# Attention written out batch by batch, values projected with tokens on the output partitions, gate products in two halves of the array

## The chip, the cores and the metric

The kernel runs on one core of a Trainium2 chip. The metric is the device time of one execution in microseconds (us); the median of several executions is compared. The engines are TensorE (PE, with its weight loads as PEld), VectorE (DVE), ScalarE (ACT), GpSimd (POOL) and SyncE (SP), which here issues DMAs.

## What is computed

Two layers on x of 8 batches x 512 tokens x 256, all in float32. `ctx` has the same shape. Each layer adds a mixer with the context and then a feed-forward part:

```python
x = x + mlstm_mix(layernorm(x), ctx, ctx, gates, outnorm)      # 4 heads of 64
x = x + gelu(layernorm(x) @ w1 + b1) @ w2 + b2                 # 256 -> 1024 -> 256
x = x + attention(layernorm(x), ctx, ctx, Wq, Wk, Wv, Wo, Bq, Bk, Bv, Bo)
x = x + expert_mlp(layernorm(x), gate_w, w1, w2)               # 8 experts, 512 tokens each

# attention: 16 heads of 64
q = query @ Wq + Bq; k = key @ Wk + Bk; v = value @ Wv + Bv     # each 256 -> 1024
probs = softmax(q_h @ k_h.T / 8)                               # per batch and head, 512 x 512
out = concat_h(probs @ v_h) @ Wo + Bo

# gates of the mixer, before the recurrence over tokens
igate = concat(q, k, v) @ ig_kernel + ig_bias                  # 4 heads, q = layernorm(x), k = v = ctx
fgate = concat(q, k, v) @ fg_kernel + fg_bias
```

## The kernel before, in words

The engines' programs are written out by hand, with semaphores between them. The stages follow each other with a barrier between: `setup` (constants), `mlstm_gates` (loads x and ctx, turns both so that features lie on partitions, gate products), `mix_and_mlp` (mixer and feed-forward part, straight code, batch by batch), `attention`, `logits`, `router`, `experts`.

**Gate stage.** PE transposes context and normalized x of a batch (`turn`, L216 and L224), ACT copies both out of PSUM, and `gate_maps` (L234) multiplies 64 columns of gate weights with 512 tokens, four steps of 128 features. The weights of batch i are shifted so that its 8 gate rows fall on rows of their own; all batches accumulate into the same 64 rows of one PSUM bank. Batch i is turned ahead of the gate product of batch i-1. At the end ACT reads rows 32 to 63 and 0 to 31 with the bias (L274, L276), and DVE and ACT work through a chain of row operations of 32x512 (L323 to L341) to the end of the stage. DVE's statistics (L58) and the normalization (L73) feed the transposes; the reciprocal root is POOL's (L85).

**Attention.** A unit u is one batch and one pair of heads, 64 in all; the pair changes slowest (`b = u % B`). The work of a unit goes in steps j = 0 to 7 (head j // 4, 128 queries each):
- PE: the score of step j (L925, two fp32r products with 512 columns), the transposes (L936) of the probabilities of step j-2 (at j = 0 and 1 those of steps 6 and 7 of the unit before). After them come, at j = 0, 1 and 4, the query, key and value products of unit u+1 (L906); at j = 2 the products of values and probabilities of unit u-1 (L947, the two heads on two halves of the array's columns); at j = 5 and 6 the output products (L957); at j = 7 the transposes of the values of unit u+1 (L914).
- DVE: row maximum (L1071), reciprocal of the row sum (L1076), copies of turned probabilities (L1083), the low parts of queries and keys (L1054, L1061); at j = 7 the two additions to x (L1089) and the copy of the turned values (L1066).
- ACT: exponential (L1015), queries and keys with bias (L990, L997), values with bias (L1003), the copy of the heads' output (L1010), and two of eight copies of turned probabilities (L1027).
- POOL: scales the probabilities (L1044).
- SP: copies the keys within the on-chip memory, four transfers of 256 KB a unit (L876), once ACT and DVE have written both parts.

There are two score banks in PSUM, so the score of step j waits for the exponential of step j-2. Queries and values share bank 4; keys and turned values share bank 5.

The weights of one pair of heads are on chip at a time. SP loads the next pair's into `w_next` and `b_next`, and every eight units DVE copies and scales them (`switch_weights`, L1093 to L1096), for which PE's next query product waits. The units run in hardware loops on every engine (`every_unit`), so their addresses and semaphore counts are computed from loop registers.

```python
for j in range(NBL):                       # PE, unit u
    score(u, par, j, first); turn(u, j - 2, first)     # at j < 2: turn(u - 1, 6 + j)
    if j in (0, 1, 4): project(u + 1, min(j, 2))
    if j == 2: weigh_values(u - 1, ...)
    if j in (5, 6): output(u - 1, j - 5)
    if j == 7: turn_values(u + 1)
```

## Time and profile before

| | us |
|---|---|
| median of 3 executions | 2006.98 |
| lowest and highest | 1998.52, 2008.62 |
| the profiled execution | 2001.98 |
| its span, first to last instruction | 2000.3 |
| gate stage, to DVE's last instruction | 73.1 |
| mixer and feed-forward part, to the next stage's first issue | 459.55 |
| attention, to DVE's last addition | 1690.8 |

The stages' ends are read from the timeline. The page gives for each engine its busy time, its share of the span and the number of instructions; a granted clock of 1.00 is 2.4 GHz for PE, 0.50 is 1.2 GHz. Ends of matmuls are modelled, so the distance from start to start tells more than a duration. A float32 product is two PE instructions, a float32 transpose and an fp32r product are one.

### The profile page before, as it was taken

Reading aid. Unit: us, or ns where it says so; the run is one execution under the profiler, and the core shown is the slowest. Engines: PE = TensorE matmul, PEld = TensorE weight load, DVE = VectorE, ACT = ScalarE, POOL = GpSimd, SP = SyncE. Lnnn points to the kernel's source line nnn. Section 1 sums busy time; section 2 is a strip of 40 time slices with the busy share of each in tenths; the row PEclk is TensorE's granted clock in tenths of the full one; section 3 lists DMA queues with packets and bytes.
Section 4 is the critical chain, followed back from the end, with each engine's and each line's share of the span. In section 5 each row is a group of like instructions: output and inputs, shape, how many; then the busy total and the mean of one; then the engine's idle time right before and its main releaser. Section 6 shows DMA issues by size and latency. Waiting matters only on the chain. (4 is left out here: it accounts for less than half of the span.)

```text
span 2000.3 us, 29128 instructions
## 1 busy us (share of the span) xinstructions
PE 1750.8 (88%) x8415; PEld 1135.9 (57%) x8415; DVE 1257.7 (63%) x2832; ACT 846.0 (42%) x1870; POOL 644.8 (32%) x761
## 2 busy tenths in 40 slices
PE   7579999995999999999999999999999997721674
PEld 4356777673666666666566566566566564721453
DVE  5444544424777777777777777777777775567341
ACT  3324333423555555555555555555555552200211
POOL 2153444421222232232232222222222222102675
PEclk9769999997999999999999999999999998555877
DMA  7000000003213213213223223223222221501443
GB/s 240 11 22 11 12 11 1 1 0 79 64 43 72 63 42 71 63 42 71 58 47 71 58 47 71 58 46 71 59 46 63 60 46 27 169 0 43 81 80 53
DMA packets 71815, 108.51 MB, mean 54 GB/s; under 512 B 16712, under 2 KB 54096, under 8 KB 71760
## 3 DMA queue, kind: packets, MB, share of 16 engines
q1 hardware_dynamic: 65616, 99.29, 20.2%
q0 software_dynamic: 6144, 8.52, 2.7%
q8 instruction: 29, 0.48, 0.1%
q14 instruction: 26, 0.21, 0.0%
HBM read 27.84 MB, written 12.85 MB: 20 GB/s over the span
## 5 line engine op out<-in xcount | busy, mean ns | idle before, releaser
L1044 POOL TENSOR_SCALAR at_Pr<-at_Pr,at_rinv 128x512 f32<-128x512 f32 x512 | 354.2, 692 | 867.6 <-DVE at_rinv L1076 867.6
L1015 ACT ACTIVATE at_Pr<-at_ps,at_nmax 128x512 f32<-128x512 f32 x512 | 351.9, 687 | 546.3 <-DVE at_nmax L1071 464.0
L925 PE MATMUL at_ps<-at_k,at_q 128*128 128x512 f32 x1024 | 439.7, 510 | 7.2 <-DMA at_k<-at_k_own 4.8
L1071 DVE TENSOR_REDUCE at_nmax<-at_ps 128x1 f32<-128x512 f32 x512 | 353.1, 690 | 114.6 <-PE at_ps L925 104.7
L936 PE MATMUL at_ps<-k_ident,at_Pr 128*128 128x128 f32 x2048 | 307.8, 273 | 4.2 <-POOL at_Pr L1044 4.2
L936 PEld LDWEIGHTS at_ps<-k_ident,at_Pr 128*128 128x128 f32 x2048 | 250.5, 140 | 84.4 <-issue 18.8
L925 PEld LDWEIGHTS at_ps<-at_k,at_q 128*128 128x128 f32 x1024 | 179.4, 191 | 157.2 <-issue 95.9
L1083 DVE COPY at_PT<-at_ps 128x512 f32<-128x512 f32 x384 | 261.0, 680 | 0.0
L906 PE MATMUL at_ps<-m_ctxT,at_w 128*128 (+1 forms) x512 | 242.2, 595 | 0.3 <-DVE at_q L1054 0.3
L947 PE MATMUL at_ps<-at_PT,at_V 128*64 128x512 f32 x1024 | 237.2, 606 | 0.9 <-DVE at_PT L1083 0.9
L1076 DVE RECIPROCAL at_rinv<-at_rsum 128x1 f32<-128x1 f32 x512 | 83.2, 163 | 179.3 <-ACT at_Pr L1015 177.3
L906 PE MATMUL at_ps<-m_xnT,at_w 128*128 (+1 forms) x256 | 126.4, 618 | 24.4 <-DVE at_w L1096 24.4
L947 PEld LDWEIGHTS at_ps<-at_PT,at_V 128*64 128x64 f32 x1024 | 68.5, 138 | 124.0 <-issue 122.9
L957 PE MATMUL at_ps<-at_wo,at_oT 128*128 (+1 forms) x512 | 131.7, 380 | 0.7 <-ACT at_oT L1010 0.7
L906 PEld LDWEIGHTS at_ps<-m_ctxT,at_w 128*128 128x128 f32 x512 | 88.1, 192 | 64.2 <-issue 62.8
L428 PE MATMUL mm_ps<-mx_w,mm_hT 128*128 128x256 f32 x512 | 120.9, 382 | 0.0
L418 PE MATMUL mm_ps<-m_xnT,mx_w 128*128 128x512 f32 x256 | 114.2, 605 | 1.3 <-ACT m_xnT L571 1.3
L428 PEld LDWEIGHTS mm_ps<-mx_w,mm_hT 128*128 128x128 f32 x512 | 93.8, 190 | 16.6 <-issue 5.3
L1054 DVE SCALAR_TENSOR_TENSOR at_q<-at_ps,at_b,at_q 64x512 fp32r<-64x512 f32 x128 | 96.0, 750 | 8.6 <-ACT at_q L990 5.7
L1015 ACT ACTIVATION_READ_ACCUMULATOR at_Pr<-at_ps,at_nmax 128x1 f32 x512 | 98.7, 193 | 0.0
L990 ACT ACTIVATE at_q<-at_ps,at_b 64x512 fp32r<-64x512 f32 x128 | 86.7, 677 | 17.9 <-PE at_ps L906 17.1
L957 PEld LDWEIGHTS at_ps<-at_wo,at_oT 128*128 128x128 f32 x512 | 87.4, 191 | 8.2 <-ACT at_oT L1010 1.6
(245 smaller groups left out, 2049.1 us busy)
## 6 DMA issues: line engine op xcount, KB each, us to landing
at_k<-at_k_own SPq DMA_DIRECT2D x256, 256.0 KB, 4.3
k_x<-in_x SPq DMA_DIRECT2D x8, 512.0 KB, 8.6
mg_ctx<-in_ctx SPq DMA_DIRECT2D x8, 512.0 KB, 8.7
mx_ctxn<-in_ctx SPq DMA_DIRECT2D x8, 512.0 KB, 3.6
rows<-lo_xn SPq DMA_DIRECT2D x8, 512.0 KB, 3.0
out<-k_x SPq DMA_DIRECT2D x1, 4096.0 KB, 14.7
ex_w_in<-in_L_ffn_w SPq DMA_DIRECT2D x16, 256.0 KB, 2.9
mx_w<-in_L_ffn_w SPq DMA_DIRECT2D x2, 1024.0 KB, 10.0
```

Source lines behind the costliest of these rows:

```text
L418: ins = pe.matmul(ps[:, H_BANK + f % 4, :], w1_s[:, k, P * f:P * f + P], xnT_all[:, k, b * S:b * S + S], start=k == 0, stop=k == DC - 1)
L428: ins = pe.matmul(ps[:, Y_BANK + t // 2, D * (t % 2):D * (t % 2) + D], hT[:, f, P * t:P * t + P], w2_s[:, f, :], start=f == 0, stop=f == F ...
L906: ins = pe.matmul(ps[:, A_BANK + k % 2, :], w_s[:, k, d, :], src[:, d, ds(b * S, S)], start=d == 0, stop=d == DC - 1)
L925: ins = pe.matmul(ps[:, S_BANK + j % 2, :], q2[:, par, h, q:q + P], k2[:, par, h, part, :], start=part == 0, stop=part == 1)
L936: ins = pe.transpose(ps[:, T_BANK + j % 2, P * t:P * t + P], Pr[:, j % 4, P * t:P * t + P], c["ident"][:, :])
L947: ins = pe.matmul(ps[AD * h:AD * h + AD, O_BANK, :], V[:, par, t, AD * h:AD * h + AD], PT[:, par, h, t, :], start=t == 0, stop=t == TPB - 1)
L957: ins = pe.matmul(ps[:, Y_BANK - half, D * (t % 2):D * (t % 2) + D], oT[:, P * t:P * t + P], wo_s[:, ds(u // B, 1), :].rearrange("p a d -> ...
L1015: act.activation(Pr[:, j % 4, :], ps[:, S_BANK + j % 2, :], ACT.Exp, bias=nmax[:, j % 4:j % 4 + 1], accum_out=rsum[:, j % 4:j % 4 + 1]).th ...
L1044: pool.tensor_scalar(Pr[:, j % 4, :], Pr[:, j % 4, :], rinv[:, j % 4:j % 4 + 1], 1.0, ALU.mult, ALU.mult).then_inc(s["pn"], 1)
L1054: ins = dve.scalar_tensor_tensor(out=q2[other, par, h, :], in0=ps[own, A_BANK, :], scalar=b_s[own, 0:1], in1=q2[own, par, h, :], op0=ALU.a ...
L1071: dve.tensor_reduce(nmax[:, j % 4:j % 4 + 1], ps[:, S_BANK + j % 2, :], AX.X, ALU.max, negate=True).then_inc(s["nmax"], 1)
L1083: dve.tensor_copy(PT[:, par, j // TPB, :, q:q + P], ps[:, T_BANK + j % 2, :].rearrange("p (t q) -> p t q", t=TPB)).then_inc(s["pt_v"], 1)
```

## The change

- Gates: `gate_maps` takes a pair of batches; the even one's product goes to PSUM rows 0 to 63, the odd one's to rows 64 to 127, in turn. DVE adds the second half's rows to fg and ig before it uses them.
- Weights: the first pair's query, key and value weights and all biases are loaded at the start of `mix_and_mlp` (`load_first`); those of the other seven pairs at the start of `attention`, in three transfers ahead of the output weights. DVE scales the query weights twice in all. `w_next`, `b_next` and `switch_weights` are gone.
- Order: the pair of heads changes fastest (`b, hp = u // HP, u % HP`), and all 64 units are straight code on every engine.
- Values: the context is the stationary operand and the weights move, so that tokens lie on the output partitions: eight products with 128 columns take the place of two with 512. The four transposes L914, ACT's copy to `vT` and DVE's copy L1066 are gone; ACT copies the bank to V at j = 5. The value bias is added to the heads' output instead (the probabilities of a row sum to 1).
- Waits: PE waits for the additions to x before `weigh_values`, DVE for its own earlier additions before the next.
- The zeros for the spare rows are written in `logits` instead of `setup`.

```diff
-                def gate_maps(i):
+                def gate_maps(pair):
+                    pe.wait_ge(s["ctxT"], 2 * pair + 2)
+                    pe.wait_ge(s["xnT"], 2 * pair + 2)
                     for k in range(2 * DC):
+                        for half in range(2):
+                            i = 2 * pair + half
+                            rhs = (xnT_all if k < DC else ctxT_all)[:, k % DC, i * S:i * S + S]
+                            at = R - MH - MH * i
+                            out = slice(2 * R * half, 2 * R * half + 2 * R)
+                            ins = pe.matmul(ps[out, GATE_BANK, :], gate_w[:, k, at:at + 2 * R], rhs,
+                                            start=pair == 0 and k == 0, stop=i >= B - 2 and k == 2 * DC - 1)
...
                 turn(0)
+                turn(1)
                 pe.wait_ge(s["gw"], 5)
-                for i in range(1, B):
-                    turn(i)
-                    gate_maps(i - 1)
-                gate_maps(B - 1)
+                for pair in range(1, B // 2):
+                    turn(2 * pair)
+                    gate_maps(pair - 1)
+                    turn(2 * pair + 1)
+                gate_maps(B // 2 - 1)
...
                 dve.wait_ge(s["fg"], 1)
+                dve.tensor_tensor(fg[:, :], ps[3 * R:4 * R, GATE_BANK, :], fg[:, :], ALU.add).then_inc(s["summed"], 1)
+                dve.wait_ge(s["summed"], 1)
...
                 dve.wait_ge(s["ig"], 1)
+                dve.tensor_tensor(ig[:, :], ps[2 * R:3 * R, GATE_BANK, :], ig[:, :], ALU.add).then_inc(s["summed"], 1)
+                dve.wait_ge(s["summed"], 2)
...
+def load_first(sp, first, Ws, bs):
+    for k in range(3):
+        sp.dma_start(first["w"][:, k, :, :], Ws[k].rearrange("(c p) n -> p c n", p=P)[:, :, 0:P]
+                     ).then_inc(first["loaded"], 16)
+        sp.dma_start(first["b"][:, k, :], bs[k].rearrange("(a p) -> p a", p=P), allow_slow_non_contiguous=True
+                     ).then_inc(first["loaded"], 16)
...
             @block.sync
             def _(sp):
+                for k in range(3):
+                    sp.dma_start(w_rest[:, k, :, :], w_dram[k][:, :, P:HP * P]).then_inc(s["w"], 16)
+                sp.wait_ge(first["loaded"], 16 * 6)
+                sp.dma_start(wo_s[:, :, :], wo_dram).then_inc(first["loaded"], 16)
+                for u in range(U):
                     sp.wait_ge(s["kh"], u + 1)
                     sp.wait_ge(s["kl"], u + 1)
...
-                    b = u % B
+                    b, hp = u // HP, u % HP
                     if k == 0:
-                        pe.wait_ge(s["scaled"], u // B + 1)
-                        pe.wait_ge(s["vT"], u)
-                    elif k == 1:
-                        pe.wait_ge(s["V"], u)
+                        wait_count(pe, s["V"], u)
                     else:
-                        pe.wait_ge(s["ql"], u + 1)
+                        wait_count(pe, s["kl"], u)
...
-                def turn_values(u):
-                    pe.wait_ge(s["vT"], u + 1)
-                    pe.wait_ge(s["kl"], u + 1)
+                def project_values(u):
+                    b, hp = u // HP, u % HP
+                    pe.wait_ge(s["ql"], u + 1)
                     for t in range(TPB):
-                        ins = pe.transpose(ps[:, A_BANK + 1, P * t:P * t + P], vT[:, P * t:P * t + P], c["ident"][:, :])
-                    ins.then_inc(s["vturned"], 1)
+                        for d in range(DC):
+                            ins = pe.matmul(ps[:, A_BANK, P * t:P * t + P],
+                                            ctxT_all[:, d, b * S + P * t:b * S + P * t + P], weights(2, d, hp),
+                                            start=d == 0, stop=d == DC - 1)
+                    ins.then_inc(s["v_ps"], 1)
...
+                def weigh_values(u):
+                    wait_turned_copies(pe, u, NBL)
+                    pe.wait_ge(s["V"], u + 1)
+                    wait_count(pe, s["x"], 2 * u)
...
                 def values(u):
                     act.wait_ge(s["v_ps"], u + 1)
-                    act.wait_ge(s["vturned"], u)
-                    act.activation(vT[:, :], ps[:, A_BANK, :], ACT.Identity, bias=b_s[:, 2:3]).then_inc(s["vT"], 1)
+                    act.copy(V[:, u % 2, :, :], ps[:, A_BANK, :].rearrange("p (t d) -> p t d", t=TPB)
+                             ).then_inc(s["V"], 1)
+
+                def heads_out(u):
+                    act.wait_ge(s["pv"], u + 1)
+                    act.activation(oT[:, :], ps[:, O_BANK, :], ACT.Identity, bias=b_s[:, 2, u % HP:u % HP + 1]
+                                   ).then_inc(s["oT"], 1)
...
-                def values(u, par):
-                    dve.wait_ge(s["vturned"], u + 1)
-                    dve.tensor_copy(V[:, par, :, :], ps[:, A_BANK + 1, :].rearrange("p (t d) -> p t d", t=TPB)
-                                    ).then_inc(s["V"], 1)
...
+                dve.wait_ge(first["loaded"], 16 * 6)
+                dve.tensor_scalar(b_s[:, 0, :], b_s[:, 0, :], AD ** -0.5, None, ALU.mult)
+                dve.tensor_scalar(w_first[:, 0, :, :], w_first[:, 0, :, :], AD ** -0.5, None, ALU.mult
+                                  ).then_inc(s["scaled"], 1)
+                dve.wait_ge(s["scaled"], 1)
+                queries(0)
+                keys(0)
+                dve.wait_ge(s["w"], 16 * 3)
+                dve.tensor_scalar(w_rest[:, 0, :, :], w_rest[:, 0, :, :], AD ** -0.5, None, ALU.mult
+                                  ).then_inc(s["scaled"], 1)
+                for u in range(U + 1):
                     for j in range(NBL):
...
```

## Rows read from the trace of the kernel before

**Rows 1.** The page, part 1: engine, busy us, share of the span, instructions.
```profile
PE 1750.8 (88%) x8415; PEld 1135.9 (57%) x8415; DVE 1257.7 (63%) x2832; ACT 846.0 (42%) x1870; POOL 644.8 (32%) x761
```

**Rows 2.** Windows, inside attention: us, each engine's busy us, clock, DMA share, GB/s.
```profile
1080.00:1677.00 597.00, 586.33 (x2800) 362.28 (x2799) 451.44 (x904) 319.97 (x731) 176.87 (x256) 1.00 0.25 57
```

**Rows 3.** Timeline, a plain unit, PE: start us, us, engine, line, operation, count.
```profile
1003.32 0.60 PE L936 MATMUL at_ps<-k_ident,at_Pr 128*128 128x128 f32 x4
1003.76 0.60 PE L914 MATMUL at_ps<-k_ident,at_vT 128*128 128x128 f32 x4
...
1006.42 1.04 PE L925 MATMUL at_ps<-at_k,at_q 128*128 128x512 f32 x2
...
1007.30 0.60 PE L936 MATMUL at_ps<-k_ident,at_Pr 128*128 128x128 f32 x4
...
1009.05 1.03 PE L925 MATMUL at_ps<-at_k,at_q 128*128 128x512 f32 x2
...
1010.03 0.63 PE L936 MATMUL at_ps<-k_ident,at_Pr 128*128 128x128 f32 x4
...
1024.89 1.04 PE L925 MATMUL at_ps<-at_k,at_q 128*128 128x512 f32 x2
```

**Rows 4.** Waits of PE from 500 to 1660 us: us in total, times, longest us.
```profile
PE at_ps L906 <- DVE at_w L1096: 17.6, 7, 2.5
```

**Rows 5.** Timeline, gate stage, PE: one batch.
```profile
46.12 1.09 PE L216 MATMUL mg_ps<-k_ident,mg_ctx 128*128 128x128 f32 x8
...
48.01 1.93 PE L234 MATMUL mg_ps<-m_xnT,mg_gate_w 128*64 128x512 f32 x4
...
51.59 1.09 PE L216 MATMUL mg_ps<-k_ident,mg_ctx 128*128 128x128 f32 x8
```

**Rows 6.** Timeline, attention, PE: values and probabilities on two halves of the array.
```profile
1010.58 3.65 PE L947 MATMUL at_ps<-at_PT,at_V 128*64 128x512 f32 x16
```

**Rows 7.** Timeline, gate stage: DVE's statistics, then the chain of rows after the products.
```profile
25.94 1.41 DVE L58 BATCH_NORM_STATS2 mg_stats<-k_x 128x6 f32<-128x256 f32 x4
...
29.42 1.41 DVE L58 BATCH_NORM_STATS2 mg_stats<-k_x 128x6 f32<-128x256 f32 x4
...
60.67 0.68 ACT L274 ACTIVATE mg_fg<-mg_ps,mg_gbias 32x512 f32<-32x512 f32 x1 [5.90 <-PE mg_ps L234]
...
66.72 0.68 DVE L330 TENSOR_TENSOR mg_g<-mg_ig,mg_cums 32x512 f32<-32x512 f32 x1
```

**Rows 8.** Timeline, entry to attention; last, the page's part 6 (KB, us to landing).
```profile
459.55 0.37 SPq L867 DMA_DIRECT2D at_w_next<-in_L_xattn_W_Query  x1
...
480.16 1.19 PE L925 MATMUL at_ps<-at_k,at_q 128*128 128x512 f32 x2 [4.79 <-DMA at_k<-at_k_own]
...
out<-k_x SPq DMA_DIRECT2D x1, 4096.0 KB, 14.7
```

**Rows 9.** Timeline, mixer: products with 130 columns; then one weight load of L906.
```profile
253.85 1.61 PE L447 MATMUL mm_ps<-mm_vaug,mm_kw 128*128 128x130 f32 x12
255.30 1.89 PE L428 MATMUL mm_ps<-mx_w,mm_hT 128*128 128x256 f32 x8
...
1005.53 0.19 PEld L906 LDWEIGHTS at_ps<-m_xnT,at_w 128*128 128x128 f32 x1 [0.24 <-issue]
```

**Rows 10.** Timeline: POOL's scaling and the transposes that read it, twice.
```profile
1003.63 0.69 POOL L1044 TENSOR_SCALAR at_Pr<-at_Pr,at_rinv 128x512 f32<-128x512 f32 x1 [1.08 <-DVE at_rinv L1076]
...
1004.67 0.60 PE L936 MATMUL at_ps<-k_ident,at_Pr 128*128 128x128 f32 x4
...
1678.13 0.69 POOL L1044 TENSOR_SCALAR at_Pr<-at_Pr,at_rinv 128x512 f32<-128x512 f32 x1 [0.90 <-DVE at_rinv L1076]
...
1678.88 0.66 PE L936 MATMUL at_ps<-k_ident,at_Pr 128*128 128x128 f32 x4 [0.60 <-POOL at_Pr L1044]
```

**Rows 11.** Mixer, 150 to 450 us: instruction packets, MB, share; the window, as in rows 2.
```profile
q8 instruction: 11, 0.18, 0.3%
...
150.00:450.00 300.00, 300.00 (x1493) 213.49 (x1492) 124.64 (x302) 111.92 (x225) 123.76 (x103) 1.00 0.02 6
```

More of the change, by code:

```diff
@@ L793, in _, with attention @@
                     step(b)
-def attention(nc, c, x_all, xnT_all, ctxT_all, Wq, Wk, Wv, Wo, Bq, Bk, Bv):
+def attention(nc, c, x_all, xnT_all, ctxT_all, first, Wq, Wk, Wv, Wo):
     U = HP * B
@@ L932, in turn @@
                         wait_turned_copies(pe, u, j - 1)
-                    elif not first:
+                    elif u:
                         wait_turned_copies(pe, u - 1, NBL - 1 + j)
@@ L1087, in add_out @@
                     dve.wait_ge(s["y_ps"], 2 * u + half + 1)
[L1088 removed]
+                    at = (u // HP) * TPB + 2 * half
+                    xv = x_all[:, at:at + 2, :].rearrange("p t d -> p (t d)")
                     dve.tensor_tensor(xv, ps[:, Y_BANK - half, :], xv, ALU.add).then_inc(s["x"], 1)
[L1091 to L1099 removed]
+                dve.wait_ge(first["loaded"], 16 * 6)
[3 more added lines that the diff above has]
+                dve.wait_ge(s["scaled"], 1)
+                queries(0)
+                keys(0)
+                dve.wait_ge(s["w"], 16 * 3)
+                dve.tensor_scalar(w_rest[:, 0, :, :], w_rest[:, 0, :, :], AD ** -0.5, None, ALU.mult
+                                  ).then_inc(s["scaled"], 1)
+                for u in range(U + 1):
                     for j in range(NBL):
[L1101 removed]
+                        if there(u):
                             if j >= 1:
@@ L1188, in step @@
                     norm_apply_dve(dve, s, i, x_all, tmp[par], wait_free)
+                dve.memset(zeros[:, :], 0.0).then_inc(s["zero"], 1)
                 dve.wait_ge(s["gT_ps"], 1)
@@ L1753, in build @@
             xnT_all = sbm("xnT", [P, DC, N], F32)
+            first = {"w": sbm("w_first", [P, 3, DC, P], F32), "b": sbm("b_all", [P, 3, HP], F32),
+                     "loaded": mid.enter_context(nc.semaphore("m_loaded"))}
             with ExitStack() as mix:
@@ L1778, in build @@
             lg = allocator(mid, nc, "r")("lg", [P, NT, E], F32)
-            logits(nc, c, landed, x_all, a["L1_ffn_gate_w"], rows, lg, out)
+            logits(nc, c, landed, x_all, a["L1_ffn_gate_w"], rows, lg, out, zeros)
             router(nc, c, lg, rows, prob, final, chunk, slot)
```

280 lines of the change are left out of this document (106 added, 174 removed).

## The prediction

> **What bounds the kernel now.** I read the page first, then the stages, then single units. The page has TensorE (PE) busy for 88% of the span [rows 1]. The windows by stage say where that binds: from 1080 to 1677 us, inside attention, PE is busy for 586.33 of 597 us at a granted clock of 1.00, VectorE (DVE) for 451 and ScalarE (ACT) for 320 [rows 2]. So attention, some 1200 of 2000 us, goes by what PE must stream, and a DVE or ACT instruction less is worth something only where PE waits for it.
>
> A unit is one batch and one pair of heads; there are 64. From the score of j=1 at 1006.42 to the same one a unit later at 1024.89 pass 18.47 us [rows 3]. At the change of weights, once in eight units, PE waits for L1096: 17.6 us in seven waits [rows 4]. In the gate stage PE sets the pace too: one batch takes 5.47 us (46.12 to 51.59), of which its gate product holds 3.58 (48.01 to 51.59) [rows 5].
>
> **Gate products in halves.** A batch's product is eight instructions of 64 output columns one after another, 0.45 us each [rows 5]. L947 has the same shape (128 rows, 64 columns, 512 moving), in turn on two halves of the array, and its 16 instructions take 3.65 us [rows 6]: two side by side. So two batches will cost 3.5 us instead of 7. DVE becomes nearly as late as PE: its statistics come every 3.48 us (25.94, 29.42) [rows 7]. I place the steps by these durations: batch 2 turned at 23.3, products done 26.9; batches 3 and 4 turned 30.3, products 33.9; 5 and 6 (waiting for DVE) 37.6, products 41.1; batch 7 turned and copied by ACT 44.2; last products 47.7. Today ACT reads the result at 60.67 [rows 7], so that is 12.8 us earlier. Added are two DVE additions of 32x512, each like L330's 0.68 us [rows 7] with a semaphore, and both lie in the chain of rows that follows: +1.45. Net -11.3; bounds +1.5 (no two side by side) and -14.
>
> **Entry to attention.** The first weights come a stage earlier, so PE can begin as soon as the stage does. But SP now issues 2.75 MB of further weights and 1 MB of output weights ahead of the first doubling of keys, 1 MB, and the first score needs that. The row for a 4096 KB store says 14.7 us [rows 8], so 4.75 MB take 17.5; from the stage's first issue at 459.55 that is 477.0, against the first score at 480.16 [rows 8]: -3, bounds 0 and -5. DVE's wait for the further weights and its scaling of them end inside that. The six small loads at the head of the mixer's SP queue are ahead of context batch 2 only, which that stage doesn't want for tens of us: nothing, and some 3 us if it did.
>
> **Weight switches.** All seven go, and with them the waits of [rows 4]: -17.6. PE sat idle in each, so nothing hides them.
>
> **The unit itself.** PE loses the four transposes of L914: four such take 0.44 us (L936 at 1003.32, then L914 at 1003.76) [rows 3]. The value product was four instructions with 512 moving columns at the pace of L947's pairs, 3.65/8 with the start, 0.43 without: 1.72 us. It becomes 16 with 128 moving columns. The nearest row has 12 instructions with 130 columns and weights of full height, 253.85 to 255.30, 0.121 us each with the first one's start [rows 9]; from below it is 0.109, the transposes' pace [rows 3]. So 1.74 to 1.93; I take 1.78, near the lower end because the start is paid once: +0.06.
>
> DVE loses L1066, 0.68 us. It stands ahead of the row maximum of j=0, and through that the transposes at j=2 are late: from score to transposes pass 0.98 us there (1009.05 to 1010.03) against 0.88 at j=1 (1006.42 to 1007.30) [rows 3]. That 0.10 goes. ACT trades one 128x512 instruction with a bias for a plain one later in the unit and puts the bias on another; at 320 of 597 us [rows 2] it has room.
>
> But something is late next. The transposes at j=0 (1004.67) read what POOL scales from 1003.63 to 1004.32 [rows 10]. That chain hangs on the score of j=6, not on L914. With L914 gone, PE wants them at 1004.23. Where PE does wait for POOL, near the end of attention, it starts 0.06 us after it (1678.13 + 0.69, then 1678.88) [rows 10], here at 1004.38, and a first instruction whose weights weren't loaded ahead costs some 0.03 more. So 0.18 of the 0.44 comes back as a new wait.
>
> Sum for a unit: -0.44 + 0.06 - 0.10 + 0.18 = -0.30; times 63, -18.9. Bounds: 0 (all given back) and -0.55 (no new wait, and smoother starts).
>
> The added waits (PE ahead of L947, DVE ahead of L1089) are for work a unit old: behind PE's stand its products and transposes for j=2, behind DVE's the next row maximum, but both are met long before. The same x is now updated in eight consecutive units, 18 us apart. One memset moves from the setup, where POOL is later anyway, to the routing stage, 0.3 us there at most.
>
> The Trainium skill speaks against the small products. Its page "TensorE: Matmul & The Clock Gate", section "The mechanism", says that weight loads overlap running matmuls only where the row group differs. By that rule 16 full-height loads would all show. The 12 full-height instructions of L447 follow each other at 0.121 us [rows 9], so here the trace disagrees; the price is rival E.
>
> **Sum.** -11.3 - 3 - 17.6 - 18.9 = -50.8. The profiled execution took 2001.98 us (span 2000.3), so 1951.2; the median of the three runs, 2006.98, lies 5.0 above it, so the forecast is 1956. Routing and experts are untouched; their granted clock changes between its levels and may move the end by some us.
>
> **Rivals.** (A) PE saves it all: -0.55 a unit instead of -0.30, 16 us more: 1940. For: PE is the bound in 98% of attention. Against: POOL's end at 1004.32 [rows 10].
>
> (B) The chain of maximum, exponential and POOL swallows the whole unit gain: +19, 1975. For: PE waits for POOL wherever it has little else, as at 1678.88 [rows 10]. Against: only one of eight groups of transposes is that near.
>
> (C) The halves don't run side by side: the gate stage gains nothing and pays 1.45: 1969. Against: L947 [rows 6].
>
> (D) Slower, by code. Attention's loops become straight code, about 12,300 weight loads and products on PE. The mixer is straight already: in 300 us it fetched 11 large instruction packets for 1493 products and as many loads [rows 11], so attention fetches some 45. The 11 took 0.3% of 16 queues' 300 us, 1.3 us each. If each stopped PE, that is +59, and with some 12 for the other engines 2027. It outweighs the gain from 1.1 us a packet. Against: in those 300 us PE was busy for 300 [rows 11], so all were hidden.
> The Trainium skill's page "Runtime: NRT & Kernel Launch", section "Instruction fetch mechanics", says that sequential code is fetched ahead while the current block runs; the mixer's row agrees.
>
> (E) Slower, by weight loads: each small product shows its load of 0.19 us [rows 9] instead of a pace of 0.11: 16 x 0.08 x 64 = +82, 2038. It outweighs the gain from 0.16 us an instruction. Against: L447's pace [rows 9].
>
> **Chances.** Forecast 0.47, A 0.24, B 0.18, C 0.04, D 0.04, E 0.03. The range leaves out D and E and the far ends of A and B: 1936 to 1978. Half a per cent, 10 us, is about what a measurement of this kernel can tell from no change. Faster by more: 0.92; within: 0.02; slower: 0.06.
>
> **What would show it.** ACT reads the gate result near 48 instead of 60.67. First score near 477 less the 11 us of the gate stage. From one unit to the next 18.2 us, with none near 21. Small value products at 0.109 to 0.121 us. A wait of PE for POOL at the j=0 transposes. Some 45 large instruction packets with no PE gap beside them. The forecast is wrong if the unit stays at 18.4 (B), is at 17.9 (A), or is above 19 (D, E).

## The result, and the profile after

The kernel after takes 1950.68 us (median of 4 executions, 1943.8 to 1953.4) beside 2007.33 us for the kernel before in the same session: a ratio of 0.972, 95% interval 0.969 to 0.975. A second session gave 1955.48 beside 2003.64, 0.974 (0.973 to 0.976). The forecast was 1956, with a range of 1936 to 1978.

The profiled execution of after took 1943.80 us, span 1942.0, and is the shortest of its set; that of before took 2001.98. Between the two lie 58.2 us. The page of after, part 1, answers to [rows 1]; behind it a line of part 3 (DMA queue, kind: packets, MB, share of 16 engines' span):

```profile
PE 1713.6 (88%) x8927; PEld 1166.4 (60%) x8927; DVE 1208.7 (62%) x2741; ACT 842.5 (43%) x1870; POOL 642.4 (33%) x761
...
q8 instruction: 71, 1.16, 0.3%
```

The share of PE is the same 88%, over a span 58 us shorter; it says nothing of where the time went. The stages do. Each begins with the first instruction that the trace has of it:

| stage | before, us | after, us | difference | forecast |
|---|---|---|---|---|
| setup and gates | 73.4 | 64.1 | -9.3 | -11.3 |
| mixer, feed-forward | 386.2 | 383.2 | -3.0 | 0 |
| attention, to its first score | 20.6 | 17.8 | -2.8 | -3 |
| attention, first score to that of unit 63 | 1179.05 | 1142.52 | -36.5 | -17.6 - 18.9 |
| attention, the rest | 31.8 | 30.7 | -1.1 | 0 |
| logits and router | 134.8 | 134.7 | -0.1 | 0 |
| experts | 174.4 | 168.9 | -5.5 | 0 |

The four lines that belong to the change come to -49.7, against -50.8 in the forecast. A second profile of the kernel after, read in the same way against the same profile of before, gives -9.0, -2.7, -35.4 and -0.3, together -47.4. So the sum itself is known to some 2 us. The mixer's and the experts' -8.5 are put down to these two executions and not to the change, for reasons that come further down.

Inside attention the windows answer to [rows 2] (us, busy us of PE, PEld, DVE, ACT, POOL, clock, DMA share, GB/s):

```profile
1080.00:1600.00 520.00, 520.00 (x2740) 341.58 (x2739) 383.54 (x773) 288.14 (x659) 158.38 (x229) 1.00 0.26 58
```

PE is busy for all of it, against 586.33 of 597 before. The plain unit answers to [rows 3] (timeline of PE: start us, us, engine, line, operation, count):

```profile
990.21 0.72 PE L905 MATMUL at_ps<-at_k,at_q 128*128 128x512 f32 x2
990.89 0.66 PE L916 MATMUL at_ps<-k_ident,at_Pr 128*128 128x128 f32 x4
...
992.70 1.03 PE L905 MATMUL at_ps<-at_k,at_q 128*128 128x512 f32 x2
...
995.33 1.03 PE L905 MATMUL at_ps<-at_k,at_q 128*128 128x512 f32 x2
996.19 0.60 PE L916 MATMUL at_ps<-k_ident,at_Pr 128*128 128x128 f32 x4
...
1001.22 0.71 PE L905 MATMUL at_ps<-at_k,at_q 128*128 128x512 f32 x2
...
1002.20 1.95 PE L893 MATMUL at_ps<-at_w_rest,m_ctxT 128*128 128x128 f32 x16
1003.91 0.71 PE L905 MATMUL at_ps<-at_k,at_q 128*128 128x512 f32 x2
1004.46 0.60 PE L916 MATMUL at_ps<-k_ident,at_Pr 128*128 128x128 f32 x4
...
1005.57 0.82 PE L905 MATMUL at_ps<-at_k,at_q 128*128 128x512 f32 x2
...
1007.35 0.82 PE L905 MATMUL at_ps<-at_k,at_q 128*128 128x512 f32 x2
...
1008.36 0.71 PE L905 MATMUL at_ps<-at_k,at_q 128*128 128x512 f32 x2
```

From the score of step 0 at 990.21 to the next at 1008.36 pass 18.15 us; the units from the third on all take 18.14 to 18.18. The L914 of before is gone. L893 is the value product, 16 instructions. At step 2 the transposes follow their score after 0.86 us (995.33 to 996.19), where [rows 3] had 0.98. At step 0 they follow after 0.68 (990.21 to 990.89), where the kernel before had 0.56. POOL, in the same timeline, shows why, and so do the waits from 500 to 1600 us (us in total, times, longest):

```profile
990.15 0.69 POOL L1018 TENSOR_SCALAR at_Pr<-at_Pr,at_rinv 128x512 f32<-128x512 f32 x1 [1.08 <-DVE at_rinv L1045]
```

```profile
PEld at_ps L916 <- POOL at_Pr L1018: 24.8, 61, 0.4
```

The scaling ends at 990.84 and the transposes start at 990.89. This wait comes in nearly each unit, 61 times here: it is the one that the forecast said would take the place of L914. No line of these waits names the copying of weights any more, as [rows 4] did.

### The profile page after: what moved, and what is told of

Same layout as the page of the kernel before. It is cut to its first block and busy times, and to the rows that moved or that the text cites. A ratio compares the mean times of both kernels' runs of the same rounds, so it can differ in the third digit from the quotient of the medians.

```text
span 1942.0 us, 26422 instructions
## 1 busy us (share of the span) xinstructions
PE 1713.6 (88%) x8927; PEld 1166.4 (60%) x8927; DVE 1208.7 (62%) x2741; ACT 842.5 (43%) x1870; POOL 642.4 (33%) x761
## 5 line engine op out<-in xcount | busy, mean ns | idle before, releaser
L905 PE MATMUL at_ps<-at_k,at_q 128*128 128x512 f32 x1024 | 420.6, 492 | 10.1 <-DMA at_k<-at_k_own 8.4
L905 PEld LDWEIGHTS at_ps<-at_k,at_q 128*128 128x128 f32 x1024 | 174.6, 191 | 129.4 <-issue 120.0
L1045 DVE RECIPROCAL at_rinv<-at_rsum 128x1 f32<-128x1 f32 x512 | 83.3, 163 | 174.4 <-ACT at_Pr L997 172.4
L936 PE MATMUL at_ps<-at_wo,at_oT 128*128 128x256 f32 x512 | 131.7, 380 | 0.8 <-ACT at_oT L983 0.8
L893 PE MATMUL at_ps<-at_w_rest,m_ctxT 128*128 128x128 f32 x896 | 109.2, 275 | 0.0
L884 PE MATMUL at_ps<-m_xnT,at_w_rest 128*128 128x512 f32 x224 | 106.6, 599 | 0.0
L884 PE MATMUL at_ps<-m_ctxT,at_w_rest 128*128 128x512 f32 x224 | 105.4, 593 | 0.0
L893 PEld LDWEIGHTS at_ps<-at_w_rest,m_ctxT 128*128 128x128 f32 x896 | 104.5, 192 | 0.0
L1027 DVE SCALAR_TENSOR_TENSOR at_q<-at_ps,m_b_all,at_q 64x512 fp32r<-64x512 f32 x128 | 95.9, 750 | 8.6 <-ACT at_q L966 5.7
```

The costliest lines, as they stand in the source:

```text
L884: ins = pe.matmul(ps[:, A_BANK + k, :], weights(k, d, hp), src[:, d, b * S:b * S + S], start=d == 0, stop=d == DC - 1)
L893: ins = pe.matmul(ps[:, A_BANK, P * t:P * t + P], ctxT_all[:, d, b * S + P * t:b * S + P * t + P], weights(2, d, hp), start=d == 0, stop=d ...
L905: ins = pe.matmul(ps[:, S_BANK + j % 2, :], q2[:, u % 2, h, q:q + P], k2[:, u % 2, h, part, :], start=part == 0, stop=part == 1)
L936: ins = pe.matmul(ps[:, Y_BANK - half, D * (t % 2):D * (t % 2) + D], oT[:, P * t:P * t + P], wo_s[:, u % HP, :], start=True, stop=True)
```

## Experiments

All times are medians. The kernel before was run beside each set; it took 2005.13 us beside the first four, 2004.78 beside the next four and 2003.64 beside the last two. "A unit" is the time from the score of step 0 to that of the next unit.

### The gate stage alone

```diff
 # the kernel before, with the halves of the kernel after
+for half in range(2):
+    i = 2 * pair + half
+    out = slice(2 * R * half, 2 * R * half + 2 * R)
+    ins = pe.matmul(ps[out, GATE_BANK, :], gate_w[:, k, at:at + 2 * R], rhs, ...)
 ...
+dve.tensor_tensor(fg[:, :], ps[3 * R:4 * R, GATE_BANK, :], fg[:, :], ALU.add)
+dve.tensor_tensor(ig[:, :], ps[2 * R:3 * R, GATE_BANK, :], ig[:, :], ALU.add)
```

> The kernel before with nothing but the gate products in halves (two batches side by side in the 128 output partitions, two additions of the halves on VectorE). The kernel after reads the gate result at 49.95 us instead of 60.67 and starts the mixer at 64.23 instead of 73.49. If those 9.3 us are the halves alone (my theory), this kernel does the same: result read at 50, mixer at 64, time 9 to 10 us under the kernel before (ratio 0.995). The two additions show as 0.69 us each. Rival: part of the gain comes from elsewhere in the changed program (one memset less at the start, other DMAs): then the result is read 1 us or more later than 49.95. Rival C of the prediction (halves don't run side by side): result at about 61, time 1.5 us over the kernel before. The attention of this kernel is untouched: units of 18.3 to 18.5 us.

Measured: 1995.24 us, ratio 0.995 (0.994 to 0.997), 9.9 us less than before. The mixer starts at 63.9. The timeline has the last product and the reading, as [rows 7] had for the kernel before (in brackets: idle before, and what ended it):

```profile
45.99 1.94 PE L237 MATMUL mg_ps<-m_xnT,mg_gate_w 128*64 128x512 f32 x8 [1.36 <-ACT m_xnT L274]
47.73 1.92 PE L237 MATMUL mg_ps<-m_ctxT,mg_gate_w 128*64 128x512 f32 x8
49.75 0.68 ACT L279 ACTIVATE mg_fg<-mg_ps,mg_gbias 32x512 f32<-32x512 f32 x1 [3.90 <-PE mg_ps L237]
...
50.46 0.69 DVE L328 TENSOR_TENSOR mg_fg<-mg_ps,mg_fg 32x512 f32<-32x512 f32 x1 [12.31 <-ACT mg_fg L279]
...
56.53 0.69 DVE L337 TENSOR_TENSOR mg_ig<-mg_ps,mg_ig 32x512 f32<-32x512 f32 x1
```

Eight instructions start 1.74 us before the next eight: 0.22 each, where one at a time they took 0.45 [rows 5]. So they do run side by side, rival C is out, and the gate stage's gain is the halves' alone. Ahead of the last product PE stands still for 1.36 us, until ACT has copied the last batch out. The forecast had that wait in its placing: it gave the last turn and its copy 3.1 us (41.1 to 44.2), where the turn alone takes 1.9.

### The value path undone

```diff
 # the kernel after, with the value path of before
-for t in range(TPB):
-    for d in range(DC):
-        ins = pe.matmul(ps[:, A_BANK, P * t:P * t + P],
-                        ctxT_all[:, d, b * S + P * t:b * S + P * t + P], weights(2, d, hp), ...)
+for d in range(DC):
+    ins = pe.matmul(ps[:, A_BANK, :], weights(2, d, hp), ctxT_all[:, d, b * S:b * S + S], ...)
 ...
+# j == 7: transposes of the values to A_BANK + 1, then DVE's copy into V; ACT's bias as before
```

> The kernel after with the old way of the values: projected with the weights resident (4 instructions of 512 columns instead of 16 of 128), biased by ScalarE, turned by 4 transposes at step 7, copied by VectorE. (There is room on chip for the weights of seven head pairs only beside the extra buffer, so the last pair computes with those of the sixth step before it; the work is the same in kind and number.) Theory: the 0.26 us by which a plain unit fell (18.42 to 18.16) is the value path alone, so units come back to 18.4, every one of them, with no longer unit where head pairs change; the wait of the step-0 transposes for the Pool half of the scaling goes away again; score 0 to score 63 is 1142.5 + 63 x 0.26 = 1159 us, and the time is 16 us over that of the kernel after, about 1967. Rival: straight code and batch order gave part of the 0.26 (loop branches, dynamic addresses): units of 18.16 to 18.3, time 1951 to 1960.

Measured: 1962.61 us (0.979, 0.978 to 0.981), units of 18.33 almost without exception, 1154.04 us from the first score to that of unit 63. So the value path is worth 0.17 a unit and not 0.26, and 11.5 us in all by the traces. The medians, 1962.61 and 1950.68, are 12 apart, but come from two sessions. At step 0 the transposes follow their score after 0.55 us again. Neither theory had it right. The value path is most of the 0.26 but not all of it, and the rival's numbers were off too. Some 0.1 us a unit had to come from what this kernel still shares with the kernel after.

### The loops written out

```diff
 # the kernel before
-with eng.Fori(0, HP - 1) as hp:
+for hp in range(HP - 1):
 ...
-with eng.Fori(0, B // 2 - 2) as pair:
+for pair in range(B // 2 - 2):
```

> The kernel before with its attention loops written out by the host (same order by head pair, same weight switches, same value path). Theory: the loops cost nothing that the end sees, because each engine's queue runs ahead of its waits; plain units stay at 18.3 to 18.5, the unit in which the weights are switched stays at about 21, time within 0.2% of the kernel before (2003 to 2011). Rival 1: the loops (register arithmetic and branches on the tensor queue, seven outer passes) cost part of what the change won: plain units 18.1 to 18.3 and a switch unit under 21, time 1990 to 2000. Rival 2 (D of the prediction): straight code must be fetched in time and is not always: PE gaps with instruction packets before them, time over 2015.

Measured: 1999.41 us, ratio 0.997 (0.996 to 0.998), 5.7 us less. Every plain unit takes 18.31 us. In the kernel before, 33 of 54 plain units (four of each eight, and five behind the last switch) take 18.46 and the others 18.32, 18.41 on average. (The expectation of the run with the moved copy, further down, has this as 5 of 8 units.) So the missing 0.1 us is the loops', and my theory that they cost nothing fell. The difference sits in one place. From the score of step 2 to its transposes pass 0.98 us in the units of 18.46, and 0.87 in those of 18.32 and in all of this kernel. The timeline of DVE in the kernel before, ahead of that, in a unit of the first sort:

```profile
986.61 0.16 DVE L1076 RECIPROCAL at_rinv<-at_rsum 128x1 f32<-128x1 f32 x1 [0.84 <-ACT at_Pr L1015]
986.90 1.29 DVE L1089 TENSOR_TENSOR k_x<-at_ps,k_x 128x512 f32 x2
988.11 0.68 DVE L1066 COPY at_V<-at_ps 128x512 f32<-128x512 f32 x1
988.70 0.68 DVE L1071 TENSOR_REDUCE at_nmax<-at_ps 128x1 f32<-128x512 f32 x1
```

and with the loops written out:

```profile
991.34 0.17 DVE L1076 RECIPROCAL at_rinv<-at_rsum 128x1 f32<-128x1 f32 x1 [0.84 <-ACT at_Pr L1015]
991.42 1.27 DVE L1089 TENSOR_TENSOR k_x<-at_ps,k_x 128x512 f32<-128x512 f32 x2
992.61 0.68 DVE L1066 COPY at_V<-at_ps 128x512 f32<-128x512 f32 x1
993.21 0.68 DVE L1071 TENSOR_REDUCE at_nmax<-at_ps 128x1 f32<-128x512 f32 x1
```

From the start of the reciprocal to that of the first addition pass 0.29 us in the loop and 0.08 in straight code. The trace has a register instruction of DVE for L1089 in that gap, 0.125 us long: the address into x is worked out from the loop register. In that profile it stands there in each of the 33 units of 18.46 us and in none of the others. The row maximum, and with it exponential, scaling and transposes, come that much later.

The same run speaks against rival D too. The 47 and 42 instruction packets of its attention (39 more on the first queue over the whole span than in the kernel before) stop nothing. And it shows a price of the weight switches that the forecast lacked. PE waits at each for about 2.5 us; in four of the seven the granted clock falls behind the wait (windows, columns as above):

```profile
616.00:618.00 2.00, 1.48 (x2) 0.84 (x3) 1.75 (x5) 0.78 (x2) 0.00 (x0) 0.52 0.03 8
618.00:620.00 2.00, 2.00 (x4) 0.83 (x3) 0.08 (x1) 0.00 (x1) 0.69 (x1) 0.63 0.00 0
620.00:622.00 2.00, 2.00 (x10) 1.17 (x9) 1.51 (x3) 1.96 (x4) 0.00 (x0) 1.00 0.00 0
```

From 614 to 616 PE was busy for 0.06 us at a clock of 1.00. In the next two windows the mean is 0.52 and 0.63, so most of these 4 us ran at 1.2 GHz, and by 620 it is back at 2.4. Such a unit takes 22.5 to 22.7 us instead of 21.05. In the profile of the kernel before it was one of seven (22.57).

### The query product ahead of the transposes

```diff
 # the kernel after, PE
+if j == 0 and there(u + 1):
+    project(u + 1, 0)
 if j < 2 and there(u - 1):
     turn(u - 1, NBL - 2 + j)
-if j < 2 and there(u + 1):
-    project(u + 1, j)
+if j == 1 and there(u + 1):
+    project(u + 1, 1)
```

> The kernel after with one pair of steps exchanged in the tensor queue: the query product of the next unit is issued ahead of the transposes of step 6 of the unit before, instead of behind them. Theory: the new wait of these transposes for the scaling on Pool (score to transposes 0.68 us against 0.56, so 0.12 a unit) has 0.86 us of product in front of it and goes; nothing else is late, units of 18.04, score 0 to score 63 about 1135, time 7.5 us under the kernel after (about 1943). Rival: the wait only moves: the transposes of step 6 come 0.86 us later, their copies free the bank for step 0 and 1 later, and the transposes of step 7 or the second score wait instead; units of 18.16 or more, time 1950 or more.

Measured: 1939.94 us (0.967, 0.966 to 0.969), units of 17.97, 1131.39 us from first score to that of unit 63. The gain is 0.19 a unit where 0.12 was expected, 11.1 us by the trace against the first profile of the kernel after, 12.3 against the second. Step 0 and step 1 of a unit now look like this:

```profile
996.17 0.72 PE L905 MATMUL at_ps<-at_k,at_q 128*128 128x512 f32 x2
996.73 1.88 PE L884 MATMUL at_ps<-m_xnT,at_w_rest 128*128 128x512 f32 x4
998.44 0.60 PE L916 MATMUL at_ps<-k_ident,at_Pr 128*128 128x128 f32 x4
998.80 0.71 PE L905 MATMUL at_ps<-at_k,at_q 128*128 128x512 f32 x2
999.35 0.60 PE L916 MATMUL at_ps<-k_ident,at_Pr 128*128 128x128 f32 x4
```

From the score of step 0 to the transposes of step 1 pass 3.18 us (996.17 to 999.35). In the kernel after they are 3.36 (990.21 to 993.57) and with the loops written out 3.17. So the order itself costs and gives nothing: the 0.19 is the wait. I had counted only the 0.12 that the transposes start later; those that waited also take 0.66 instead of 0.60, and all behind them moves by that too.

### Pool's scaling cut short

```diff
 # the kernel after, Pool
+w = P if n % NBL == NBL - 2 else S
-pool.tensor_scalar(Pr[:, n % 4, :], Pr[:, n % 4, :], ...)
+pool.tensor_scalar(Pr[:, n % 4, 0:w], Pr[:, n % 4, 0:w], ...)
```

> The kernel after in which Pool scales only 128 of the 512 columns for step 6 of each unit (three quarters of that scaling are left out; nothing else differs, the tensor queue is untouched). It tells what moving the query product ahead (units of 17.97) took away: theory, the wait of the step-0 transposes for Pool and nothing more, so a shorter scaling of that step does the same: score to transposes 0.55 instead of 0.68, units of 17.97. Rival: a part of the 0.19 came from the new order itself (a long product behind a score instead of behind transposes); then these units fall only by 0.12, to 18.04. A miss of the whole idea: they stay at 18.16, and the copies of the turned tiles set the time.

Measured: one execution of 1943.34 us, where the profiled execution with the query product ahead took 1943.05; units of 17.97 and 17.98, 0.55 us from score to transposes at step 0. The order of PE's queue is untouched here, so the 0.19 us is the wait for POOL. The rival with 18.04 is out.

### Keys doubled first

```diff
 # the kernel after, SP
-for k in range(3):
-    sp.dma_start(w_rest[:, k, :, :], w_dram[k][:, :, P:HP * P])
-sp.dma_start(wo_s[:, :, :], wo_dram)
 for u in range(U):
+    # u == 0: the weights of pair 1; u == 1: those of pairs 2 to 7; u == 2: the output weights
     sp.wait_ge(s["kh"], u + 1)
     sp.wait_ge(s["kl"], u + 1)
```

> The kernel after with its loads at the entry of attention in another order: only the weights of the second head pair (0.375 MB) are issued ahead of the first doubling of keys, the others between the first and the second doubling, the output weights between the second and the third. Theory: the first score waits for the 1 MB of keys behind 3.375 MB of weights (the doubling is issued at 455.50, the score starts at 465.11); with the queue empty it lands some 6 us after its issue, so the first score comes 14.0 to 14.5 us after the stage's first issue instead of 17.8, units as before at 18.16 and the time 3 to 4 us under the kernel after (about 1947). Rival: the bytes are only moved: the second doubling is then late, the first or second unit is longer than its 16.25 and 18.54 by what was won, time 1950 to 1951.

The timeline of the entry:

```profile
457.62 0.37 SPq L868 DMA_DIRECT2D at_w_rest<-in_L_xattn_W_Query  x1
...
465.51 3.17 SPq L873 DMA_DIRECT2D at_k<-at_k_own  x4
...
472.46 1.19 PE L911 MATMUL at_ps<-at_k,at_q 128*128 128x512 f32 x2 [5.74 <-DMA at_k<-at_k_own]
```

The first score comes 14.8 us after the stage's first issue. In three other profiles with the old order it is 17.8 to 18.4 (kernel after twice, gate order). From the issue of the doubling to the first score pass 7 us instead of 9.6. The first two units take 16.99 and 18.68 us; in the two later profiles with the old order, the kernel after again and gate order, they take 16.99 and 18.53 or 18.54. So the rival, by which they take the gain back, is out but for 0.1 us. Attention as a whole takes 1190.1 us here against 1193.1 and 1193.5 in those two: 3 us, in place as the theory had it and at the lower end of its 3 to 4. The first profile of the kernel after has 1191.1, as its first unit (16.25) and the end of attention were shorter by 0.7 and 0.8 us, for which I have no cause. The times don't show the 3 us surely: 1951.65 us (0.974, 0.972 to 0.975) lies between the two medians of the kernel after. The mixer, below, varies by more than that.

### The last batch of the gate stage turned earlier

```diff
 # the kernel after, PE
 for pair in range(1, B // 2):
     turn(2 * pair)
+    if pair == B // 2 - 1:
+        turn(2 * pair + 1)
     gate_maps(pair - 1)
-    turn(2 * pair + 1)
+    if pair < B // 2 - 1:
+        turn(2 * pair + 1)
```

> The kernel after with the last batch of the gate stage turned ahead of the third pair's gate product instead of behind it. Theory: the last product waits 1.36 us for ScalarE's copy of the turned last batch; with 3.6 us of product between them that wait goes: gate result read at 48.6 instead of 49.95, mixer at 62.9 instead of 64.23, time 1.3 us less, which the times can't tell (1945 to 1953) and the trace can. Rival: the statistics on VectorE or the copies on ScalarE set the pace of the last turn, which then waits itself: 49.9 as before or later.

Measured: 1955.05 us (0.975, 0.973 to 0.977), not to be told from the kernel after, as both theories had it. In the trace the last four groups of products follow each other without a wait, and the result is read at 49.01 instead of 49.95; the mixer starts at 63.2 instead of 64.1. It is 0.9 us, not 1.3: the third turn in a row waits another 0.28 us for ACT's copy, so the rival holds in part.

### The copy of the values behind the row maximum

```diff
 # the kernel before, DVE
 row_max(u, j)
+if j == 0 and not first and not drain:
+    values(u, par)
 ...
 if j == 7:
     ...
-    if ahead:
-        values(u + 1, 1 - par)
```

> The kernel before with VectorE's copy of the values moved from ahead of the first row maximum of a unit to behind it; loops, switches and all else as before. In the kernel before 5 of 8 units take 18.46 us and the others 18.32; the 0.14 is the transposes of step 2, 0.98 instead of 0.87 us after their score. In these units register arithmetic for the dynamic address of the output addition holds VectorE 0.18 us ahead of the copy; the same loops written out have 18.31 throughout. Theory: the lateness needs both, the arithmetic and the copy, in front of the row maximum; with the copy (0.68 us) behind it, all plain units take 18.31 to 18.33 with the loops still there, and the time is some 5 us under the kernel before. Rival: the loops cost it on another engine (tensor queue, Pool), so the units stay at 18.46 and the time too.

Measured: 2007.37 us, 1.0015 (1.0003 to 1.0028): 2.6 us slower. Half of the theory held. The transposes of step 2 follow their score after 0.87 us in every unit, with the loops still there. So the lateness of the kernel before needed both the address arithmetic and the copy: written-out loops remove it with the copy in place, and the moved copy removes it with the loops in place. But plain units took 18.4 to 18.65. What I had overlooked is who waits for the copy (waits from 500 to 1660 us; then the timeline, DVE's copy and PE):

```profile
PEld at_ps L906 <- DVE at_V L1066: 2.0, 8, 0.3
```

```profile
992.02 0.68 DVE L1066 COPY at_V<-at_ps 128x512 f32<-128x512 f32 x1
...
992.15 0.60 PE L936 MATMUL at_ps<-k_ident,at_Pr 128*128 128x128 f32 x4
...
992.83 1.95 PE L906 MATMUL at_ps<-m_ctxT,at_w 128*128 x4
```

The key product shares its bank with the turned values. The view names eight such waits; in the unit shown the copy ends at 992.70 and the product starts at 992.83. It now starts 0.68 us behind the transposes of step 1, against 0.43 in the kernel before (1007.30 to 1007.73 there). A wait of 0.1 at step 2 was traded for one of 0.1 to 0.3 at step 1. The address arithmetic still counts there, since it delays the copy: the 33 plain units that have it take 18.58 to 18.65 us, and 19 of the 21 without it take 18.38 to 18.45. The seven switch units became 0.6 us shorter, 20.5 instead of 21.1. From the first score to that of unit 63 pass 1182.6 us instead of 1179.05.

### The kernel after again, and the three reorderings together

> The kernel after once more, unchanged, beside the combined version on one chip. Theory: its runs lie at 1944 to 1956 with units of 18.16; what moves them is the granted clock in the first 80 us of the mixer, where the same instructions took 383.1 us for the mixer in one execution (clock back at full level from 125 us) and 393.4 in another (from 138 us). Rival: the low time of the first profile was particular to that program on that chip and the mixer takes 390 or more here in all runs; then the median is 1951 to 1955.

> The kernel after with three reorderings: query product ahead of the step-6 transposes, keys doubled ahead of most loads at the entry, last gate batch turned before the third pair's products. Theory: the three are at different places and add: 63 x 0.19 = 12.0, 3.5 at the entry, 1.1 in the gate stage, so 16 to 17 us under the kernel after run beside it, about 1934 to 1936, units of 17.97, first score 14.8 us after the stage's first issue. Rival: the first unit takes the entry's gain back when both are there (the query product now stands ahead of everything in unit 0 and the second doubling waits), so 12 to 13 us, 1938 to 1939.

The combined kernel holds the three edits shown above and nothing else. It took 1938.33 us (0.967, 0.965 to 0.968), the kernel after beside it 1955.48 (0.974, 0.973 to 0.976). So it beats the kernel after by 17.2 us, 0.9%, and the kernel before by 65. The theory had 16 to 17. By the trace attention takes 1176.5 us instead of 1193.1, with units of 17.97. The sum came out, its parts less so. The units give 12.4 as expected. The first score comes 15.8 us after the stage's first issue instead of 17.9, a gain of 2.1 where 3.5 was expected; the gate stage gives 0.4 where 1.1 was. Another 2.0 came at the end of attention, behind the score of unit 63, where nothing was expected. The first unit takes 16.80 us, against 16.99 in the kernel after, so the rival is out: it takes nothing back. The edits don't undo each other; that 17.2 is so near to 16 to 17 is in part luck. The time itself, 1938.33, lies outside the theory's 1934 to 1936, since the kernel after beside it was higher than assumed too.

For the mixer the rival was the better guide. Its instructions are the same in all kernels that start from the one after. It took 383.2 us in the first profile of the kernel after and 392.5 in the second, 392.6 to 393.4 in five of the variants and 389.9 in the sixth, the one with the old value path. (One of the five executions of the kernel after, 1948.1 us, is short again; only the profiled one can be read by stage.) Windows over its beginning, first profile, then second:

```profile
64.00:124.00 60.00, 34.95 (x208) 30.47 (x209) 27.84 (x47) 11.93 (x39) 23.54 (x23) 0.70 0.12 25
124.00:144.00 20.00, 18.75 (x55) 10.04 (x53) 5.95 (x10) 10.63 (x15) 10.72 (x9) 0.92 0.09 27
```

```profile
64.00:124.00 60.00, 35.91 (x173) 30.94 (x173) 25.85 (x45) 12.06 (x39) 22.63 (x23) 0.56 0.11 25
124.00:144.00 20.00, 17.04 (x62) 11.98 (x63) 7.96 (x14) 5.92 (x9) 7.29 (x6) 0.62 0.01 5
```

PE is busy for 35 of 60 us in both, but the granted clock is 0.70 in the one and 0.56 in the other, then 0.92 and 0.62. That is a difference of 9 us for one and the same code. It is as large as the whole gate term, and enough to hide the 3 us of the keys. The four profiles with the mixer of the kernel before have 386.2, 386.2, 392.4 and 390.2 us. The two sets overlap, so no effect of the change on the mixer is shown; one of a few us either way isn't ruled out.

## Why the prediction was right, step by step

**The bound.** Right. PE set the time of attention before and does so after, and what left PE's queue or its waits left the time, but for what came back as a new wait.

**Gate products in halves: -9.3 instead of -11.3.** The mechanism was right, shown by the run with nothing else changed. The step that was off is the placing of the batches. I had the last products done at 47.7; they end just ahead of ACT's read at 49.95, 2.2 us later. The first products are in place: done at 26.9 by the forecast, at 27.05 in the trace. Most of what was off lies in the two places with two turns in a row, for which I had 3.4 and 3.7 us. Both take 4.32. By [rows 5] one turn takes 1.89 us, so two come to 3.8, and 3.4 was too low. And between the two PE waits 0.38 us for ACT's copy of the context, which the forecast lacked; it had a wait for DVE at the second place, and there is none. The timeline of the kernel after, from the first turn to the products:

```profile
34.96 1.09 PE L215 MATMUL mg_ps<-k_ident,mg_ctx 128*128 128x128 f32 x8
...
37.30 1.06 PE L215 MATMUL mg_ps<-k_ident,mg_ctx 128*128 128x128 f32 x8 [0.38 <-ACT m_ctxT L269]
...
39.28 1.94 PE L236 MATMUL mg_ps<-m_xnT,mg_gate_w 128*64 128x512 f32 x8
```

That is 1.5 of the 2.2 us. The last turn with its copy took 3.3 us where 3.1 was forecast, the 1.36 us of standing still included, and two groups of eight take 3.6 and not 3.5. The two additions cost 1.45 us in all, as forecast: from ACT's read to the mixer pass 14.17 us (49.95 to 64.12) instead of 12.72 (60.67 to 73.39).

**Entry: -2.8 instead of -3.** Right in size. The basis, that the first keys wait in the queue behind 3.75 MB, was shown by moving most of it behind them: 3 us more were won.

**Weight switches: -21 instead of -17.6.** The seven units with a switch took 149.2 us in the profile of before; as plain units of 18.32 they would have taken 128.2. The forecast counted the wait of PE's products alone, 2.5 us each. A switch unit is 2.78 longer than a plain one, all of it between the scores of step 0 and 1. That is what the weight loads ahead of these products wait, 2.75 each (before, 500 to 1670 us):

```profile
PEld at_ps L906 <- DVE at_w L1096: 19.2, 7, 2.8
```

In one of the seven the clock fell for another 1.5.

**The unit: -15.5 instead of -18.9.** A plain unit fell from 18.41 on average to 18.16. Its parts are read from score to score, with the loops written out (the timeline below) against the kernel after (the timeline above), on average over the units of a profile:

| part | forecast | measured | from |
|---|---|---|---|
| transposes of the values gone | -0.44 | -0.42 | step 7: 1.44 to 1.02 |
| value product as 16 small ones | +0.06 | +0.08 | steps 4 and 5: 4.28 to 4.36 |
| late transposes of step 2 | -0.10 | -0.10 | units of 18.41 to 18.31, loops written out |
| new wait for POOL | +0.18 | +0.19 | step 0: 2.30 to 2.49; gone with scaling cut short or query product first |

With the loops written out, the scores of steps 0, 1, 4, 6, 7 and of the next step 0:

```profile
990.40 0.71 PE L925 MATMUL at_ps<-at_k,at_q 128*128 128x512 f32 x2
...
992.70 1.02 PE L925 MATMUL at_ps<-at_k,at_q 128*128 128x512 f32 x2
...
1001.23 0.71 PE L925 MATMUL at_ps<-at_k,at_q 128*128 128x512 f32 x2
...
1005.51 0.81 PE L925 MATMUL at_ps<-at_k,at_q 128*128 128x512 f32 x2
...
1007.27 0.81 PE L925 MATMUL at_ps<-at_k,at_q 128*128 128x512 f32 x2
...
1008.71 0.71 PE L925 MATMUL at_ps<-at_k,at_q 128*128 128x512 f32 x2
```

The four parts come to -0.25, as measured. The forecast had -0.30; the first, second and fourth parts gave 0.01 or 0.02 less than it said. Times 63 that is 15.8 us, near the 15.5 of the traces: the seven switch units, counted above from 18.32, fall by 0.16 only, and the first two units by 0.8 and 0.3. The kernel with the old value path has 18.33 where the one with the loops written out has 18.31; for these 0.02 I have no cause. The small products start 1.71 us ahead of the next score (1002.20 to 1003.91 above). A pace of 0.107 us an instruction (1.71 over 16) says that the weight loads stay hidden, so rival E is out.

The sentence of the Trainium skill that the forecast weighed (page "TensorE: Matmul & The Clock Gate", section "The mechanism") would have had them show, and this trace disagrees with it: 0.107 us for a full-height load and a product of 128 columns together. The same section also lets a load run ahead into a background buffer for weights, which I left out of the forecast; with that sentence the trace agrees.

The third line was right in size for a reason that was only half right. I put the late transposes down to DVE's copy L1066 ahead of the row maximum. It took the loop's address arithmetic as well, and either gone is enough to bring these transposes in time. The change removes both. That the average is again 0.10 is chance: it is 0.14 in 33 of 54 plain units and nothing in the others, and the forecast had read a unit of the first sort, taken its transposes to be 0.10 late and given that to all. The forecast costed the loops themselves at nothing, and so would have missed 0.10 us a unit in a change that wrote out the loops and kept the copy. The new wait was named with its place and its size, from POOL's end at 1004.32 and its row at the end of attention [rows 10]. Its 0.03 for a slower start was a guess; the transposes that waited take 0.06 longer, and start 0.13 late instead of 0.15.

**Rivals.** A (17.9 a unit) would have needed no new wait; that it is just what one gets once the wait is taken away, 17.97, was shown by two runs. B is out by the units of 18.16, C and E as said. For D, attention from 475 to 1600 us has 49 instruction packets on the first queue, near the 45 forecast, and PE is busy for 1123.8 of the 1125 us.

**The sum.** -50.8 against -49.7 for the parts. Sizes that were off pull against each other: 2.0 and 3.4 too much for the gates and the unit, 3.4 too little for the switches; 1.1 us at the end of attention were not foreseen, and the second profile has only 0.3 of them. The prediction is right within a few us, and right in its main mechanisms; that the sum comes so near is luck of this kind. By medians the kernel fell by 56.7 us in the first session and by 48.2 in the second, on either side of the sum. The clock in the mixer and the experts' stage varies by enough for that.

## What to carry to other kernels

When an instruction is taken out of the queue of the bounding engine, ask which chain on the other engines was covered by it. Here 0.19 of 0.42 us came back as a wait. An independent product moved into that place took it away again, for nothing, sixty-three times. Before moving an instruction on a helper engine, list all who wait for its result, its memory bank included: the copy that was moved away from one wait made another.

Address arithmetic of a loop counts where it stands in a chain that the bounding engine waits for: here 0.14 us a unit in the kernel before, and 0.2 when the copy behind it was moved. To see it, compare units of the same loop with each other; 18.32 and 18.46 side by side in one profile were the sign, and the forecast had read only one unit.

## What the runs showed of the hardware that was not expected

- A wait of PE of 1.9 to 2.5 us was followed by a fall of the granted clock in 7 of 28 cases (one of seven in the kernel before, one in the run of the gates alone, four with the loops written out, one with the moved copy). It costs 1.4 to 1.7 us each time. Why one case and not another is open.
- The beginning of the mixer, where PE is busy for 58 to 60% of the time, took up to 10 us more or less with the same instructions (383.2 to 393.4), and the granted clock is the one difference that the traces show. A single profile of such a stage can't be compared with another to better than that.
- The experts' stage took 174.4 us in the profile of the kernel before and 168.8 to 170.7 in the eleven other profiles, with the same code. The granted clock came up from 1.2 to 2.4 GHz some 30 us after the stage's begin there, and 26 to 27 us after it in four of the others that I looked at. That is a part of the difference; the rest is open.
